# The last linear of a graph network kernel: four of its ten node tiles by seven half-size products a pair

## The reference, cut to what matters

```
h   = relu(x @ W_self0 + mean(x) @ W_neigh0 + b0)
y   = layernorm(x + h @ W_self1 + mean(h) @ W_neigh1 + b1)
out = layernorm(y + segment_sum(norm * (y @ W.T + b)[col], row))
```

## Time and profile before

| what | value |
|---|---|
| median of 3 runs | 849.21 us (848.33 to 852.57) |
| the profiled execution | 849.59 us, of which 847.9 us are the span of the profile |
| PE (TensorE) busy | 98% of the span, 4295 matmuls |
| DVE and ACT busy | 54% and 21% of the span |
| the gather, all four chunks | from 635 to 731.7 us of the span |
| the last linear | from 731.67 to 840.62 us |
| granted clock of TensorE | 0.999 of full speed |

### The profile page before, as it was taken

How to read it: one execution, slowest core, us unless ns; L and a number is a source line. 1 busy time by engine, 2 the same in 40 slices (tenths; PEclk the granted TensorE clock), 3 DMA queues, 4 the chain that set the end, 5 groups by cost and what they waited for, 6 DMA issues and landing times.

```text
span 847.9 us, 11000 instructions
## 1 busy us (share of the span) xinstructions
PE 830.6 (98%) x4295; PEld 707.9 (83%) x4295; DVE 461.3 (54%) x714; ACT 177.4 (21%) x218; POOL 459.1 (54%) x343
## 2 busy tenths in 40 slices
PE   8999999999999999999999999999999999999996
PEld 6888888888897899788888888778889889988885
DVE  6465568200017565897544677775556435455555
ACT  4111132110111113353123112222222122200000
POOL 5028887787777887885888788788620000000000
PEclk9999999999999999999999999999999999999999
DMA  9977965463776425668876668267877649555551
GB/s 332 380 304 267 350 193 168 125 176 75 213 236 180 122 57 133 249 237 286 298 282 222 243 220 284 62 176 214 240 245 255 223 150 295 189 199 199 198 193 46
DMA packets 99480, 180.52 MB, mean 213 GB/s; under 512 B 15474, under 2 KB 75898, under 8 KB 94048
## 3 DMA queue, kind: packets, MB, share of 16 engines
q1 hardware_dynamic: 60144, 124.17, 44.0%
q10 hardware_dynamic: 26896, 40.65, 13.3%
q0 software_dynamic: 12384, 14.95, 7.6%
HBM read 107.08 MB, written 72.43 MB: 212 GB/s over the span
## 4 chain that ended last, share of the span: by engine, by line
PE 61%; POOL 15%; DMA 9%; issue 8%; DVE 5%; SPq 1%; ACT 1%; POOLq 0%; ACTq 0%; DVEq 0%
PE ps L1572 19%; POOL adj_in L643 14%; PE ps L1429 12%; PE ps L1606 10%; PE ps L1589 9%; PE ps L1515 8%; DMA adj_in<-u 4%; DMA first_rows<-in_L_gnn_W_neigh 1%; DMA spare<-in_x 1%; DMA xin<-s0t_scr 1%; PE ps L1413 1%; DVE u L914 1%; PE ps L1380 1%; SPq L514 1%; DVE sacc L1303 0%
## 5 line engine op out<-in xcount | busy, mean ns | idle before, releaser
L643 POOL DMA_INDIRECT adj_out<-loops,idx_out x160 | 245.2, 1533 | 65.4 <-issue 65.4
L643 POOL DMA_INDIRECT adj_in<-mult,idx_in x160 | 198.1, 1238 | 86.8 <-issue 86.8
L1572 PE MATMUL ps<-u 128*128 128x512 f32 x840 | 190.7, 389 | 1.4 <-DVE u L914 1.4
L1572 PEld LDWEIGHTS ps<-u 128*128 128x128 f32 x840 | 157.6, 188 | 34.2 <-issue 1.6
L1484 PE MATMUL ps<-wx 128*128 128x512 f32 (+1 forms) x576 | 109.4, 351 | 1.3 <-ACT outb L761 1.3
L1484 PEld LDWEIGHTS ps<-wx 128*128 128x128 f32 x576 | 93.9, 189 | 16.9 <-ACT outb L761 1.9
L1429 PE MATMUL ps<-u 128*128 128x512 f32 x432 | 98.2, 389 | 0.0
L1515 PE MATMUL ps<-wx,u 128*128 128x256 f32 (+5 forms) x640 | 94.8, 309 | 1.2 <-DVE ht L1191 1.2
L1589 PE MATMUL ps<-u,panel_tiles 128*128 128x512 f32 (+1 forms) x400 | 93.9, 393 | 1.9 <-DVE u L914 1.9
L1429 PEld LDWEIGHTS ps<-u 128*128 128x128 f32 x432 | 81.0, 188 | 16.8
L1515 PEld LDWEIGHTS ps<-wx,u 128*128 128x128 f32 (+1 forms) x640 | 86.6, 191 | 8.2 <-DVE ht L1191 1.6
(11 more groups left out here) (167 smaller groups left out, 779.8 us busy)
## 6 DMA issues: line engine op xcount, KB each, us to landing
left_scr<-u SPq DMA_DIRECT2D x7, 2560.0 KB, 9.5
u<-left_scr SPq DMA_DIRECT2D x7, 2560.0 KB, 9.6
xt_scr<-wx ACTq DMA_DIRECT2D x10, 1024.0 KB, 9.9
u<-xt_scr SPq DMA_DIRECT2D x10, 1024.0 KB, 5.1
wx<-xt_scr SPq DMA_DIRECT2D x16, 512.0 KB, 4.0
adj_in<-u POOLq DMA_DIRECT2D x4, 1600.0 KB, 25.3
adj_out<-u POOLq DMA_DIRECT2D x4, 1600.0 KB, 16.1
wx<-adj_in SPq DMA_DIRECT2D x5, 1280.0 KB, 7.1
```

The source lines that it names most:

```text
L643: pool.indirect_dma_start(table, bass.IndirectOffsetOnAxis(ap=index[0:EP, j:j + 1], axis=0), counts[0:EP, j:j + 1], None, bounds_check=CEL ...
L1572: ins = nc.tensor.matmul(ps[:, product_bank(g, i, p), :], left_op[n % 2][:, p, k, left, :], right_op[n % 2][:, k, right, :], start=(not on ...
```

## The change: what it does

1. **Order and products of the last linear.** The tiles go 0, 1, 8, 6, 7 as before (48 matmuls each), then the pairs (2, 3) and (4, 5), each by seven half-size products (`half_products`) of 4 feature blocks x 3 parts = 12 matmuls of 128x512, then tile 9. A pair's left matrix is 2x2 blocks: 2 tiles x 2 halves of the features.
2. **Left sums, in the gather.** In chunk 1 (tiles 2 to 5) the feature blocks go in the order 0, 4, 1, 5, 2, 6, 3, 7. After every second block, ACT copies four 128x128 quarters (two for each of two units), DVE makes five sums for each unit (`halve`), ACT the high part of seven 128x128 pieces (one instruction of 896 columns), DVE the low part (`halve_low`), and ACT issues two stores for each unit (`store_halves`, 448 KB each, in pieces of 512 bytes). There are eight units and three sets of places; set 0 and 1 are the four g_out places, set 2 is a spare piece and `bias`. A unit waits for the stores of the unit three before it. The store of gather block 7 is issued between the copies of unit 0 and 1. Scale steps and weight splits move with them: splits 1 and 2 now stand behind blocks 9 and 13.
3. **Right sums, in the last linear.** SP loads the four quarters of the weight again (1 MB each). DVE makes five sums of 128x2048 (`weight_sum`), ACT their high parts (`sum_high`), DVE their low parts (`sum_low`), between the work of the five plain tiles.
4. **Loads of the last linear.** Each half product has its own left operand (512 KB) in a ring of four places that are the two tile places; the first two are loaded when tile 6 has been multiplied, the next two when tile 7 has. Tiles 8 and 9 use another place (`late_tile`); the residual rows have four places in place of two. The bias is loaded later, behind tiles 0 and 1.
5. **Results of the pairs.** ACT copies three of the seven products from their banks (`keep_half`), DVE combines them (`pair_sums`) and adds them to the residual; the banks are used again within a pair, with accumulation.

```diff
-            for t in range(NT):
-                if t == 0:
-                    sp.wait_ge(g_full, KD * 3)
...
+            load_rest(0)
+            load_rest(1)
+            for i, (r, c) in enumerate(((0, 1), (1, 1), (0, 0), (1, 0))):
+                sp.dma_start(w_block[i], wt_scr[r * HD:(r + 1) * HD, c * HD:(c + 1) * HD].rearrange("(k p) j -> p k j", p=P)
+                             ).then_inc(block_in[i], 16)
+            for j in range(4):
+                sp.wait_ge(g_stored[j], 16 * 9)
+            sp.wait_ge(w_lo_done, KD * 3)
+            load_left(8, late_tile)
+            load_rest(8)
+            load_rest(7)
+            sp.wait_ge(acc_full, acc_index(GCN, 0) + 1)
+            load_left(6, g_tile[:, 0, :, :])
...
+            for j in range(14):
+                if j == 0:
+                    sp.wait_ge(acc_full, acc_index(GCN, 6) + 1)
+                elif j == 2:
+                    sp.wait_ge(acc_free, acc_index(GCN, 6) + 1)
+                    load_rest(4)
+                    sp.wait_ge(acc_full, acc_index(GCN, 7) + 1)
+                load_half(j)
...
+            def places_free(n):
+                if n % 3 == 2:
+                    return [(left_stored[0], 16 * (4 + 2 * (n // 3)))]
+                return [(g_stored[2 * (n % 3) + h], 16 * (2 + n // 3)) for h in range(2)]
...
             for m, (c, d) in enumerate(H_BLOCKS):
+                if c != 1:
+                    act.wait_ge(g_full, m + 1)
...
+                    if d >= 4 or c > 0:
+                        act.wait_ge(g_stored[m % 4], 16 * ((0, None, 5, 7)[c] + d // 4))
...
+                elif d % 2 == 1:
+                    two = (d - 1, d)
+                    act.wait_ge(g_full, m + 1)
+                    for n in two:
+                        lo, col = halves[n % 3][1], units[n][2] * 2 * T
+                        for free in places_free(n):
+                            act.wait_ge(*free)
+                        nc.scalar.activation(lo[:, 5, :], ps[:, g_bank(m - 1), col:col + T], ACT.Copy)
+                        nc.scalar.activation(lo[:, 6, :], ps[:, g_bank(m), col + T:col + 2 * T], ACT.Copy).then_inc(left_hi, 1)
+                        if n == 0:
+                            store_g(KD - 1)
+                    for n in two:
+                        hi, lo = halves[n % 3]
+                        act.wait_ge(left_sum, 5 + n)
+                        nc.scalar.activation(hi[:, :, :].bitcast(F32R), lo[:, :, :], ACT.Copy).then_inc(left_hi, 1)
+                    for n in two:
+                        store_halves(n)
-                if m in (4, 8, 12, 16, 20, 24):
-                    split_hi(GCN, m // 4 - 1)
+                if m in (4, 9, 13, 16, 20, 24):
+                    split_hi(GCN, (4, 9, 13, 16, 20, 24).index(m))
...
+            for q in range(2):
+                before = ((7,), (3, 2))[q]
+                root(before[0], position(before[0]))
+                keep_half(q, 0)
+                store_out(before[0])
+                keep_half(q, 1)
...
+            weight_sum(0)
+            weight_sum(1)
+            finished(0)
+            weight_sum(2)
+            add_rest(8)
+            weight_sum(3)
+            finished(1)
+            weight_sum(4)
+            sum_low(0)
+            add_rest(7)
+            finished(8)
+            sum_low(1)
+            add_rest(6)
+            sum_low(2)
+            finished(6)
+            sum_low(3)
+            finished(7)
+            sum_low(4)
...
+            def half_products(q):
+                right = [(KH, HD), (0, 0), 0, 1, 2, 3, 4]
+                for i in range(7):
+                    j = 7 * q + i
+                    pe.wait_ge(*left_landed(j))
+                    if q == 0 and i >= 2:
+                        pe.wait_ge(right_hi, 15 + right[i])
+                        pe.wait_ge(right_lo, 15 + right[i])
+                    if i == 0:
+                        pe.wait_ge(acc_free, acc_index(GCN, PAIR_BEFORE[q]) + 1)
...
+                    elif i == 2:
+                        pe.wait_ge(bank_copied, half_copied(q, 0))
+                    elif i == 4:
+                        pe.wait_ge(bank_copied, half_copied(q, 1))
+                    elif i == 5:
+                        pe.wait_ge(combined, half_read(q, 0))
+                    elif i == 6:
+                        pe.wait_ge(bank_copied, half_copied(q, 2))
+                    bank = HALF_BANKS[q][(0, 1, 0, 2, 1, 0, 2)[i]]
+                    onto = i not in (0, 1, 3)
+                    for k in range(KH):
+                        for l, r in ((0, 0), (0, 1), (1, 0)):
...
-                for t in range(NT):
+                for t in (0, 1, 8, 6, 7):
                     linear(GCN, t)
+                for q in range(2):
+                    half_products(q)
+                linear(GCN, NT - 1)
```

More of the change, by code:

```diff
@@ new lines, in store_out @@
+            def store_out(t):
+                act.wait_ge(norm_done, position(t) + 1)
+                act.dma_start(out[node_rows(t), :], outb[0:rows(t), t % 2, :]).then_inc(stored[t % 2], 16)
+            for t, sums in ((0, (0, 1)), (1, (2,)), (8, (3, 4)), (6, ())):
+                root(t, position(t))
+                store_out(t)
+                for x in sums:
+                    sum_high(x)
+            for q in range(2):
[4 more added lines that the diff above has]
+                keep_half(q, 1)
+                if q > 0:
+                    root(before[1], position(before[1]))
+                    store_out(before[1])
+                keep_half(q, 2)
@@ L903, in _ @@
+            for t in (5, 4):
+                root(t, position(t))
+                store_out(t)
+            t = NT - 1
+            root(t, position(t))
+            for n in range(2):
+                cols = slice(n * BANK, (n + 1) * BANK)
+                act.wait_ge(norm_done, position(t) + 1 + n)
+                act.dma_start(out[node_rows(t), cols], outb[0:rows(t), t % 2, cols]).then_inc(stored[t % 2], 16)
         @block.vector
@@ new lines, in outb_free, with plain @@
+                    dve.wait_ge(stored[t % 2], 16 * (NT // 2 + turn_of(t)))
+            def plain(t):
+                outb_free(t)
+                dve.wait_ge(acc_full, acc_index(GCN, t) + 1)
+                nc.vector.scalar_tensor_tensor(outb[:, t % 2, :], pair_bank(acc_pair(GCN, t))[:, :], dscale[:, t:t + 1], rest_of(t),
+                                               ALU.mult, ALU.add).then_inc(acc_free, 1)
+                dve.wait_ge(acc_free, acc_index(GCN, t) + 1)
+                for n in range(2):
+                    half_stats(t % 2, n)
@@ L1363, in _ @@
+            norm(t, position(t), BANK)
         @block.tensor
@@ L1630, in gather @@
                     ins.then_inc(scol_full, 1)
+            def half_products(q):
[8 more added lines that the diff above has]
+                        pe.wait_ge(acc_free, acc_index(GCN, PAIR_BEFORE[q]) + 1)
+                    elif i == 3 and q == 1:
+                        pe.wait_ge(sfac_done, 4)
+                    elif i == 2:
[10 more added lines that the diff above has]
+                        for l, r in ((0, 0), (0, 1), (1, 0)):
+                            if i < 2:
+                                row, col = right[i]
+                                moving = w_row(GCN, row + k, r)[:, col:col + HD]
+                            else:
+                                moving = sums_of_w[right[i]][:, k, r, :]
+                            ins = nc.tensor.matmul(ps[:, bank, :], ring[j % 4][:, k, l * T:(l + 1) * T], moving,
+                                                   start=(not onto and k == 0 and l + r == 0), stop=(k == KH - 1 and l == 1),
+                                                   skip_group_check=onto)
+                    ins.then_inc(product, 1)
             def keep_busy(n):
```

340 lines of the change are left out of this document (240 added, 100 removed).

## The result

The changed kernel takes 853.65 us (median of 11 runs, 852.03 to 856.72) against 849.94 us (848.06 to 852.57) for the kernel before, run beside it 11 times: a ratio of 1.0049, 95% interval 1.0037 to 1.0062. That is 3.7 us slower, just under the 0.5% that the prediction calls measurable, but the interval lies clear of no change. The forecast was 846.0 us and 843.3 to 851.5; the time lies 2.1 us above the range, and on the other side of the kernel before.

The account below looks back on a forecast made before the run. TensorE was taken to bound the kernel, busy in 98% of the span. -5.45 for matmuls removed, +1.9 at the last panel and +0.3 in the last linear gave -3.25 from 849.2: 846.0 us, range 843.3 to 851.5.

Parts of the forecast that it names:

- The matmuls removed: Last linear: two pairs of tiles save 24 matmuls at 0.227 us each, -5.45 us.
- the wait of +1.9 at the last panel: Gather, before chunk 3: panel issued at 706.1, landing at 715.2, needed at 713.36; +1.9 us, bounds none and 3.9.
- The half stores: Gather, chunk 1: a unit's stores land 4.6 us after issue alone, 6.0 taken for unit 2 beside loads.
- The panel's own time: Gather, load of the last chunk's panel: 9.1 us taken, from 9.1 to 11.1 in this stretch.
- the prediction's upper bound of 3.9: Wait in us before chunk 3 if the last panel's load takes 11.1 us.
- the signs of being wrong: Unit stores landing in 7 us or more, panel in under 7, or PE waiting over 1 us before the third product.
- +0.3 in front of the third product: Last linear: ACT's copy of the pair's first product ends at 791.8, needed at 791.6; bounds none and 2.3 us.
- the full gain: Rival, chance 0.33: no wait worth the name in the gather; 843.8 us, up to 844.8.
- Slower, 859 or 852 by half stores that land late: Rival, chance 0.12, of which 0.07 beyond the bound: half stores hold the gather and the last panel lands late.
- its middle case: Slower rival with each unit's stores landing 1.8 us later, the middle of L859's rows: 852 us.
- Its deciding point: Slower rival: panel landing 9.7 us late gives 853.5 us, about 2 us more per unit than assumed.

Follow-up runs that it names:

- early splits and scale steps: Changed kernel, weight splits 1 to 5 behind gather blocks 8, 9, 13, 16, 20, six scale steps of chunks 2 and 3 first on DVE: 849.1 against 851.24.
- the last kernel above: Changed kernel with splits earlier and scale steps ahead, plus sum_low(4) moved ahead of tile 7's work on DVE: 852.54 against 851.24, ratio 1.001.
- the fastest kernel: Changed kernel with splits earlier, six scale steps ahead and half stores in 3.5 KB pieces: 846.4 against 851.24 for the kernel before, ratio 0.9947.

## Why the prediction was wrong

**The matmuls removed:** right. -5.44 us for -5.45, and 168 half products in 38.08 us, 0.227 each.

**The step that failed: the wait of +1.9 at the last panel.** The mechanism was right: of the places that could bring a wait, the chain goes through the one named, by the same links. Its size was off: 9.5 us with what follows from it. In three parts:

- *The half stores.* By the prediction's coordinates less the 1.0 us by which chunk 1 began earlier, the first two pairs were on time (issued at 670.5 and 679.65, for 671.3 and 680.0), pair 3 is issued at 691.3 for 690.0, pair 4 at 701.2 for 698.7, and block 16's copy is at 704.85 for 701.8: 3.1 late. Most of it is landing. From the first issue of the unit that pair 3 waits for (679.65) until its second store had landed it took 7.8 us, where the sum had 6.0, and the last copy of pair 3 waited for it until 687.5. For pair 4 it took 6.1 (691.29 to 697.35), where the sum had 4.6. These two make the 2.5 by which pair 4 is late. The last 0.6 is issuing: the store that block 16's place hangs on had landed 3.0 us after its issue, at 704.2, and ACT was through with its four issues at 704.75. The prediction counted no time of ACT for them, and ACT was held 3.6 to 6.2 us a pair; but in pairs 3 and 4 the landing ended after the issue, so that the landing decided. That long pieces, which shorten both, bring the copy forward by 4.3 us is shown; how the 4.3 divide between the two is not, since no kernel changed one alone.
- *The panel's own time.* I took 9.1 of 9.1 to 11.1; it took 11.1. The panel issued 3.0 later and 2.0 longer on its way make the wait 6.8 in place of 1.9. The value was the lowest of its rows, with the reason that the same traffic stands beside it; there was 1.07 of DMA share in the window, against the earlier trace rows 1.00.
- *The clock.* It was in no term of the sum, nor in a rival. Behind the wait the granted clock was at the lower of its two levels, 0.50, for more than four microseconds of work, and the chunk cost 2.7 more. The kernel before with nothing but a late panel shows the same, 3.25 behind a wait of 3.2, and the other traces show it behind shorter waits too: 1.8 behind 2.9 (long pieces), 1.7 behind 2.3 (early splits and scale steps), but nothing behind a wait of 2.4 for banks in the last kernel above. The Trainium skill (TensorE: Matmul & The Clock Gate, Part 1) has the clock depend on how busy TensorE has been recently; the trace agrees, with 0.60 us of PE in 7 and 0.50 in the window after it. With the 3 us or so that it cost behind the waits of 3.2 and 6.8, the prediction's upper bound of 3.9 would have stood at about 7 (an estimate).

Together: 1.9 became 6.8 + 2.7 = 9.5, which is 7.6 more than forecast, and more than the -5.44 it was set against. Of the signs of being wrong that the prediction named, one came true: the stores of the second pair landed after 6.5 to 8.1 us, three of the four in 7 or more.

**The right end of the sum: +0.3 in front of the third product.** In the changed kernel it is 0: the copy ended at 799.53 and PE came to it at 800.22. The first weight sum began 11.8 us after the linear, for 11.6 forecast:

```profile
752.05 2.29 DVE L1078 SCALAR_TENSOR_TENSOR plain_w<-plain_w 128x2048 f32<-128x2048 f32 x1 [4.71 <-DMA plain_w<-wt_scr]
```

The working was good to a microsecond. With 13.2 us to the first weight sum and a second wait of 1.4 for the third quarter, in the fastest kernel, the same spot costs 1.8.

**The 512 bytes.** The Trainium skill (DMA: Bandwidth & Descriptors, Specifications) gives 512 bytes as enough for full line rate. Here stores in pieces of 512 bytes ran mostly at 280 to 300 GB/s again, as in the earlier trace rows, and the same bytes in pieces of 3.5 KB at about 400. So the trace goes on not to bear it out for stores, and the full gain, the rival to which that rule would lead, did not come.

**The rivals.** Slower, 859 or 852 by half stores that land late, was right in sign and half right in its means: the two landings on the path came 1.8 and 1.5 us later than assumed, about its middle case (1.8 for each unit, 852), and the panel's own load and the clock did the rest. Its deciding point, a panel that lands 9.7 us late, was too far off as well, since the clock adds to the wait: -5.44 and a wait of 6.8 sufficed for a slower kernel. The chance of 0.12 for it was too small for a stretch with so many unseen transfers.

**The long issue.** In the changed kernel two stores took 5.21 us to issue (680.67) and 2.5 to 2.8 in the other pairs. The other runs show when. In all five kernels with pieces of 512 bytes in which weight row 3 and the panel of chunk 2 (1.8 MB) are issued 3 us ahead of the second pair, the same two stores take 5.2 to 5.3 us; in the three with early splits, where that panel went out some 22 us ahead and only a weight row (0.5 MB) 3 us ahead, 2.5 to 2.6. And where the last panel goes out 3 us ahead of the fourth pair (the panel first, or early splits), its four issues take 5.8 to 6.5 us, for 3.6 in the changed kernel; with long pieces and the panel there they take 2.3 to 2.5. So in these runs the issue of short pieces took longer when a panel load had just gone out, and that of long pieces did not.

**What I call shown, and what not.** Shown by a kernel of its own: the cost of the clock behind a wait, that the panel's place makes the panel wait, that a loss of some 5 us remains without it, that splits, scale steps and long pieces together remove it all. Read from the traces alone: how block 16's delay divides between landing and issuing. Open: how much of the landing times is the short pieces and how much the loads beside them.

## What to carry to other kernels

A wait of TensorE is to be priced with what its clock does behind it: here 3.2 us of wait cost 6.4 in the traced execution, and waits of 2.3 and 2.9 cost 1.7 and 1.8 more. When work is added beside a full engine, take the landing of its stores with the loads that will be under way, count the issuing as work of the engine that does it, and follow the lists for what stands behind it: the part that saves matmuls was right to 0.01 us, and the result hung on a split of a weight row that stood behind the delayed copies and ahead of a panel load. And when a first remedy gives half, look for the step that the late ones share: of the kernels with scale steps ahead and long pieces, the one with the panel first is level with the kernel before, and the one with the splits ahead is faster. (The two differ in the place of the loads of the bias and of tile 1 too.)

## What the runs showed of the hardware

- The issue of a store of 448 KB in pieces of 512 bytes took ACT 0.37 to 2.9 us in the changed kernel, and four in a row 3.6 to 6.2 us (up to 6.5 in the others, with a panel load beside them); in pieces of 3.5 KB four took 2.3 to 2.7, with or without such a load.
- Stores ran mostly at 280 to 300 GB/s in pieces of 512 bytes and at about 400 in pieces of 3.5 KB.
- A load of 1280 KB in chunks 2 and 3 took 7.1 to 11.5 us, by what stood beside it.
- Behind waits of PE of 3.2 and 6.8 us the granted clock was 0.50 for four to six microseconds of work, which cost 3.25 and 2.7 us. In five other traces it was 0.50 for some two to four microseconds behind waits of 1.9 to 2.9 us, at a cost of 1.6 to 1.8. Behind three others, of 1.9, 2.0 and 2.4 us, and where PE did not wait, it stayed at 1.00.
